# FFN stage on one NeuronCore: the quantised rows turned by DMA from SyncE instead of by TensorE through PSUM

## The chip, the cores and the metric

One core of a Trainium2 chip. The metric is the device time of one execution in microseconds (us); lower is better.

## The reference, cut to what matters

The whole program is an attention layer and, behind it, an expert layer with a quantised FFN, each with its residual. The change lies in the last stage only, which computes, for 4096 rows of 1024 values (`x` is the sum after attention):

```python
base   = x @ W.T                                   # 1024 x 1024
gates  = top-2 softmax of x @ Wr.T + language bias  # 8 experts, rank 16
z      = base + 2 * ((x @ A.T) * gates) @ B.T
zb     = z.astype(bfloat16)
qg, sg = dynamic_quant(zb, inv_gate)               # xs = zb * inv; scale = max|xs| / 127 per row
qu, su = dynamic_quant(zb, inv_up)                 # q = clip(round(xs / scale), -127, 127)
gate   = (qg @ w_gate.T) * sg * s_wgate            # 1024 -> 512
up     = (qu @ w_up.T) * su * s_wup
inter  = clip(silu(gate) * up, -10, 10).astype(bfloat16)
qi, si = dynamic_quant(inter, inv_inter)
out    = x + (qi @ w_down.T) * si * s_wdown        # 512 -> 1024
```

## The kernel before, in words

The kernel has three stages one after the other. The attention stage and the output projection take the first 1640 us or so of the span and are not touched. The last stage, `expert_ffn_block`, works on 32 tiles of 128 rows (`TILES`), and `tile_loop` (L1018 on) writes the same body for each engine: the first four bodies (t = 0 to 3) written out, then a hardware loop of seven rounds of four bodies, then three bodies that only drain. Body t works on four tiles at once, guarded by `has(k)`: `has(0)` is the router and the splitting of x of tile t, `has(1)` the linear layer of tile t-1, `has(2)` the quantisation and the gate and up products of tile t-2, `has(3)` everything behind them of tile t-3. The order of work on an engine is the order in which the body is written, and semaphores order the engines against each other. So each engine stands still at the first wait that isn't met, with all that follows in its body behind it.

The engines and the names that the change and the prediction touch:

- SyncE (SP) issues DMAs. In body t: wait for `fin_set`, store the result of tile t-3 (L1058), then load x of tile t+1 into one of four buffers (L1035). It has nothing else to do.
- ScalarE (ACT), in this order: `zb` from PSUM to bf16, in two halves (L1114); `Sigmoid` of the gate (L1118); `x_hi`, the high part of x of tile t (L1123), which waits for the load; for i = 0 and 1 (gate, up) the rounding `xs[i] * rinv + ROUND` (L1127) and the quantised rows `qb[i]`, 128 rows x 1024 values in bf16 (L1131); the two router weights `w12` (L1134, L1135); `qi` (L1139) and `qiT` (L1142) of the down product.
- VectorE (DVE), in this order: `gt` (L1185), `xs[0]` (L1192), `ut` (L1196), the maxima and scales of the rows (L1168 to L1178), the intermediate and its quantisation (L1210 to L1220, of them `xi` L1213), the router (L1223 to L1233), the clamp of the turned rows `qT[0]`, `qT[1]` (L1238), `hg_hi` and `hg_lo` (L1242, L1244), `diag` (L1248), the gates and `hg` (L1253 to L1260), `si_sb` (L1268), and the two products that make the output `o` (L1274, L1277).
- GpSimd (POOL): `xs[1]` (L1081), two products of silu (L1084, L1087), `x_lo` (L1090), the residual `fin` (L1094).
- TensorE (PE), in this order: the first half of the linear layer of tile t-1, 24 matmuls (L1291); router and LoRA of tile t (L1307); 6 matmuls of the second half; the 16 transposes of `qb` into `q_ps` (L1318); 6 matmuls; the transpose of `hg` (L1327); the transposes of `qi` (L1332), which wait for `qi_set`; 6 matmuls; the row scales (L1342), which wait for `diag_set`; the down product, 32 matmuls (L1348); 6 matmuls; the gate product of tile t-2 (L1357), which waits for `qT_set` and `o1_set`; the LoRA product (L1370); the up product (L1357).

`q_ps` is two of the eight banks of PSUM. `qT[i]` is laid out `[128, 8, 128]`: value, chunk of 128 values, row.

Of the kernel before, what the change touches and what calls it, by code (L numbers as in the profile page):

```python
# [21 lines left out]
BF16 = mybir.dt.bfloat16  # L22
I32 = mybir.dt.int32
U32 = mybir.dt.uint32
ALU = mybir.AluOpType
# [3 lines left out]
P = 128  # L29
# [3 lines left out]
C = D // P  # L33
TILES = POS // P
# [10 lines left out]
QMAX = 127.0  # L45
# [890 lines left out]
def expert_ffn_block(nc, ctx, io, x2T, out, ident, resident):  # L936
# [11 lines left out]
    def ps(name, shape, dt=F32):  # L948
        return ctx.enter_context(nc.psum_tensor(name, shape, dt))

    def sem(name):
        return ctx.enter_context(nc.semaphore("f_" + name))
# [10 lines left out]
    ident_b = sb("ident_b", [P, P], BF16)  # L963
# [15 lines left out]
    zb = sb("zb", [P, D], BF16)  # L979

    xs = [raw[:, i] for i in range(2)]
    qb = [sb(f"qb{i}", [P, D], BF16) for i in range(2)]
    qT = [sb(f"qT{i}", [P, C, P], BF16) for i in range(2)]

    amax, rinv = sb("amax", [P, 3], F32), sb("rinv", [P, 3], F32)
    sc = sb("sc", [P, 4, 3], F32)
# [5 lines left out]
    o_sb = [raw[:, 2 + i].rearrange("p (c n) -> p c n", n=P) for i in range(2)]  # L992

    z_ps = ps("z_ps", [P, 2, HALF])
    q_ps = ps("q_ps", [P, 2, C, P], BF16)
    g_ps = ps("g_ps", [P, 2, HALF])
    s_ps = ps("small_ps", [P, HALF])
    t_ps = ps("turn_ps", [P, HALF])
# [3 lines left out]
    x_in = [sem(f"x_in{i}") for i in range(4)]  # L1002
    (b_in, dn_in, vec_in, inv_in, o_out, w_hi_set, w_lo_set, b_hi_set, b_lo_set, ident_set, iota_set, lang_set, lbias_set,
     a_mm, xh_set, xl_set, lg_set, m8_set, ix_set, gap_set, ixf_set, w12_set, g1_set, g2_set, gates_set, hc_set, hg_set,
     ht_mm, hh_set, hl_set, z_mm, zb_set, xg_set, xu_set, amax_set, sc_set, rinv_set, rnd_set, qb_set, tq_mm,
     qT_set, gu_mm, gt_set, ut_set, sg_set, p1_set, p2_set, ib_set, xi_set, iamax_set, isc_set, irinv_set,
     ird_set, icl_set, diag_set, qi_set, ti_mm, qiT_set, si_mm, si_set, d_mm, o1_set, o2_set, fin_set) = (sem(n) for n in (
        "b_in", "dn_in", "vec_in", "inv_in", "o_out", "w_hi", "w_lo", "b_hi", "b_lo", "ident", "iota", "lang", "lbias",
# [3 lines left out]
        "ird", "icl", "diag", "qi", "ti_mm", "qiT", "si_mm", "si", "d_mm", "o1", "o2", "fin"))  # L1012

    UNROLL = 4
    block = ctx.enter_context(nc.Block())

    def tile_loop(eng, body):


        for j in range(UNROLL):  # L1020
            body(j, j, lambda k, j=j: k <= j)
        with eng.Fori(1, TILES // UNROLL) as T:
            for j in range(UNROLL):
                body(T * UNROLL + j, j, lambda k: True)
        for j in range(3):
            body(TILES + j, j, lambda k, j=j: k > j)
# [5 lines left out]
    @block.sync  # L1032
    def _(sp):
        def load_x(t, j):
            sp.dma_start(x_sb[j], x2T[:, :, bass.ds(t * P, P)].rearrange("c p n -> p c n")).then_inc(x_in[j], 16)  # L1035

        load_x(0, 0)
        sp.dma_start(b_raw[:], bT[:, :]).then_inc(b_in, 16)
        with nc.allow_non_contiguous_dma(reason="1024 scales, once"):
            sp.dma_start(sd_c[:], s_down.rearrange("(c p) -> p c", p=P)).then_inc(vec_in, 16)  # L1040
        def load_vector(dst, src, done):
            sp.dma_start(dst, src.rearrange("(o n) -> o n", o=1).broadcast_to([P, dst.shape[1]])).then_inc(done, 16)

        load_vector(lang_i[:], itok, vec_in)
        load_vector(sg_all[:], s_gate, vec_in)
        load_vector(su_all[:], s_up, vec_in)
        load_vector(ii_all[:], inv_inter, vec_in)
        load_x(1, 1)
        sp.wait_ge(w_lo_set, C)
        load_vector(ig_all, inv_gate, inv_in)  # L1050
        load_vector(iu_all, inv_up, inv_in)

        def body(t, j, has):
            if has(3):
                sp.wait_ge(fin_set, t - 2)
                if not (isinstance(t, int) and t == 3):
                    sp.wait_ge(o_out, t * 16 - 48)
                sp.dma_start(out[bass.ds(t - 3, 1)].rearrange("o p n -> (o p) n"),  # L1058
                             o_sb[(j + 1) % 2].rearrange("p c n -> p (c n)")).then_inc(o_out, 16)

            if has(0) and not (isinstance(t, int) and t == 0):
                load_x((t + 1) % TILES, (j + 1) % 4)

        tile_loop(sp, body)
        sp.wait_ge(o_out, 16 * TILES)
        sp.wait_ge(x_in[0], 16 * (TILES // 4 + 1))

# [31 lines left out]
    @block.scalar  # L1099
    def _(act):  # L1100
        act.wait_ge(x_in[0], 16)
        act.activation(x_hi[0][:], x_sb[0], ACT.Identity).then_inc(xh_set, 1)
        for c in range(C):
            act.activation(w_hi[:, c], raw[:, c], ACT.Identity).then_inc(w_hi_set, 1)
        act.wait_ge(b_in, 16)
        act.activation(b_hi[:], b_raw[:], ACT.Identity).then_inc(b_hi_set, 1)

        def body(t, j, has):
            if has(2):
                act.wait_ge(xg_set, t - 2)  # L1110
                act.wait_ge(xu_set, t - 2)
                for b in range(2):
                    act.wait_ge(z_mm, t * 2 - 3 + b)
                    act.activation(zb[:, b * HALF:(b + 1) * HALF], z_ps[:, b], ACT.Copy).then_inc(zb_set, 1)  # L1114
            if has(3):
                act.wait_ge(gt_set, t - 2)
                act.wait_ge(ib_set, t - 3)
                act.activation(silu[:], gt[:], ACT.Sigmoid).then_inc(sg_set, 1)  # L1118
            if has(0) and not (isinstance(t, int) and t == 0):
                act.wait_ge(x_in[j], x_count(t, j))  # L1120
                if not (isinstance(t, int) and t < 2):
                    act.wait_ge(z_mm, t * 2 - 2)
                act.activation(x_hi[j % 2][:], x_sb[j], ACT.Identity).then_inc(xh_set, 1)  # L1123
            if has(2):
                for i in range(2):
                    act.wait_ge(rinv_set, t * 2 - 3 + i)
                    act.activation(xs[i], xs[i], ACT.Copy, bias=ROUND, scale=rinv[:, i:i + 1]).then_inc(rnd_set, 1)  # L1127
                    if i == 0 and not (isinstance(t, int) and t == 2):
                        act.wait_ge(tq_mm, t * 2 - 4)
                    act.wait_ge(rnd_set, t * 2 - 3 + i)  # L1130
                    act.activation(qb[i][:], xs[i], ACT.Copy, bias=-ROUND).then_inc(qb_set, 1)  # L1131
            if has(0):
                act.wait_ge(gap_set, t + 1)
                act.activation(w12[:, 0:1], gap[:], ACT.Sigmoid)  # L1134
                act.activation(w12[:, 1:2], gap[:], ACT.Sigmoid, scale=-1.0).then_inc(w12_set, 1)  # L1135
            if has(3):
                act.wait_ge(icl_set, t - 2)
                act.wait_ge(ti_mm, t - 3)
                act.activation(qi[:], xi[:], ACT.Copy, bias=-ROUND).then_inc(qi_set, 1)  # L1139
                act.wait_ge(ti_mm, t - 2)  # L1140
                act.wait_ge(d_mm, t - 3)
                act.activation(qiT[:], qi_ps, ACT.Copy).then_inc(qiT_set, 1)  # L1142

        tile_loop(act, body)

    @block.vector
    def _(dve):
# [8 lines left out]
        for e in range(2):  # L1156
            rows = slice(SEQ * e, SEQ * (e + 1))
            ins = dve.tensor_copy(lang[rows, :], lang_i[rows, :].rearrange("p (t e) -> p t e", e=2)[:, :, e])
# [21 lines left out]
        def body(t, j, has):  # L1180
# [51 lines left out]
                dve.wait_ge(ix_set, t + 1)  # L1232
                dve.tensor_copy(ixf[:], ix[:, 0:2]).then_inc(ixf_set, 1)  # L1233
            if has(2):
                dve.wait_ge(gu_mm, t * 2 - 4)
                for i in range(2):
                    dve.wait_ge(tq_mm, t * 2 - 3 + i)
                    dve.tensor_scalar(qT[i][:], q_ps[:, i], QMAX, -QMAX, ALU.min, ALU.max).then_inc(qT_set, 1)  # L1238
            if has(1):
                dve.wait_ge(ht_mm, t)  # L1240
                dve.wait_ge(z_mm, t * 2 - 2)
# [40 lines left out]
    def _(pe):  # L1282
# [11 lines left out]
        def body(t, j, has):  # L1294
# [7 lines left out]
            if has(0):  # L1302
# [3 lines left out]
                for c in range(C):  # L1306
                    ins = pe.matmul(h_ps, x_sb[j][:, c, :], ar_w[:, c, :], start=(c == 0), stop=(c == C - 1))  # L1307
                ins.then_inc(a_mm, 1)
            if has(1):
                if not first:  # L1310
                    pe.wait_ge(zb_set, t * 2 - 2)
                linear(one, 1, range(0, 2), first)
            if has(2):
                pe.wait_ge(qT_set, t * 2 - 4)
                for i in range(2):
                    pe.wait_ge(qb_set, t * 2 - 3 + i)
                    for c in range(C):
                        ins = pe.transpose(q_ps[:, i, c], qb[i][:, c * P:(c + 1) * P], ident_b[:])  # L1318
                    ins.then_inc(tq_mm, 1)
            if has(1):  # L1320
                linear(one, 1, range(2, 4), first)
                pe.wait_ge(hg_set, t)
# [5 lines left out]
            if has(3):  # L1328
                pe.wait_ge(ut_set, t - 2)
                pe.wait_ge(qi_set, t - 2)  # L1330
                for c in range(CI):
                    ins = pe.transpose(qi_ps[:, c], qi[:, c * P:(c + 1) * P], ident_b[:])  # L1332
# [3 lines left out]
            if has(3):  # L1336
# [9 lines left out]
                for f in range(C):  # L1346
                    for c in range(CI):
                        ins = pe.matmul(g_ps[:, f // 4, (f % 4) * P:(f % 4 + 1) * P],  # L1348
                                        dn_w[:, c, f * P:(f + 1) * P], qiT[:, c], start=(c == 0), stop=(c == CI - 1))
# [14 lines left out]
            if has(1):  # L1364
# [3 lines left out]
                for b in range(2):  # L1368
                    for k, (a, w) in enumerate(((hg_hi, b_hi), (hg_hi, b_lo), (hg_lo, b_hi))):
                        ins = pe.matmul(z_ps[:, b], a[:], w[:, b * HALF:(b + 1) * HALF],  # L1370
                                        start=False, stop=(k == 2))
# [75 lines left out]
```

## Time and profile before

| | |
|---|---|
| time, median of 3 | 2393.21 us (2391.35 to 2397.13) |
| the profiled execution | 2398.05 us, span 2396.1 us |
| busy in the span | PE 95%, PEld 77%, DVE 55%, ACT 29%, POOL 55% |
| DMA | 188.33 MB, mean 79 GB/s |
| the chain that ended last | of the span: TensorE 11%, VectorE 6%, GpSimd 6%, issue 5%, ScalarE 2% |

Times are in us from the start of the span. PE is TensorE's matmuls, PEld its weight loads, SPq the queue of SyncE's DMA instructions. A bracket at the end of a line of the timeline is the idle time of the engine before that instruction and what ended it. The chain view goes back from the last instruction, at each step to what released it; a piece in it can be shorter than the instruction, since it ends where the next piece was released.

### The profile page before, as it was taken

What the parts mean: (1) busy time and instruction counts of PE and PEld (TensorE: products, weight loads), DVE (VectorE), ACT (ScalarE), POOL (GpSimd) and SP (SyncE); (2) the same over time, 40 slices, a digit from 0 to 9 for tenths busy, and PEclk for the clock granted to TensorE, in tenths of its full rate; (3) what the DMA queues carried; (4) which work ended last, traced back from release to release, by engine and by line L of the source; (5) the groups of instructions that cost most, each with busy time, mean ns of one, the idle gap of its engine ahead of it and who ended that gap; (6) DMA issues with size and microseconds to landing.
All of it is one profiled execution on the core that took longest, in us unless ns stands there. A gap on an engine that the chain in (4) does not pass through costs nothing. (4 is left out here: it accounts for less than half of the span.)

```text
span 2396.1 us, 48171 instructions
## 1 busy us (share of the span) xinstructions
PE 2268.3 (95%) x19520; PEld 1836.1 (77%) x19552; DVE 1307.3 (55%) x2248; ACT 701.5 (29%) x1122; POOL 1319.8 (55%) x1091
## 2 busy tenths in 40 slices
PE   6999999999999999999996999998999999999996
PEld 5888877888778888788885888886777777777774
DVE  5354464445644555545455322224677777777775
ACT  3222242222422223322223101012343333333332
POOL 6887878887778786888750000001455445445443
PEclk9999999999999999999998999998999999999998
DMA  4211122111221112121116844444011111111111
GB/s 139 65 60 57 61 98 68 63 59 63 80 89 56 66 54 72 65 69 54 63 37 202 239 165 132 132 166 132 19 53 53 39 49 53 47 41 53 53 35 44
DMA packets 130374, 188.33 MB, mean 79 GB/s; under 512 B 16162, under 2 KB 61346, under 8 KB 130210
## 3 DMA queue, kind: packets, MB, share of 16 engines
q1 hardware_dynamic: 118130, 165.92, 21.7%
q10 hardware_dynamic: 9216, 16.78, 1.8%
q0 software_dynamic: 2864, 3.28, 0.8%
q8 instruction: 123, 2.02, 0.3%
q14 instruction: 41, 0.34, 0.0%
HBM read 138.76 MB, written 50.33 MB: 79 GB/s over the span
## 5 line engine op out<-in xcount | busy, mean ns | idle before, releaser
L662 PE MATMUL acc<-y_hi,w_slot_hi 128*128 128x512 f32 x1344 | 541.6, 403 | 29.8 <-DVE unit L521 9.0
L662 PE MATMUL acc<-y_hi,w_slot_lo 128*128 128x512 f32 x1344 | 528.6, 393 | 0.0
L662 PE MATMUL acc<-y_lo,w_slot_hi 128*128 128x512 f32 x1344 | 527.7, 393 | 0.0
L313 POOL TENSOR_TENSOR w_slot_lo<-w_raw,w_slot_hi 128x512 fp32r<-128x512 f32 x329 | 424.3, 1290 | 26.3
L662 PEld LDWEIGHTS acc<-y_hi,w_slot_hi 128*128 128x128 f32 x1344 | 254.7, 189 | 90.2 <-issue 27.3
L311 POOL CAST w_slot_hi<-w_raw 128x512 fp32r<-128x512 f32 x329 | 218.0, 663 | 169.2 <-PE acc L662 134.8
L662 PEld LDWEIGHTS acc<-y_hi,w_slot_lo 128*128 128x128 f32 x1344 | 254.6, 189 | 54.8
L662 PEld LDWEIGHTS acc<-y_lo,w_slot_hi 128*128 128x128 f32 x1344 | 255.1, 190 | 48.9
L316 POOL TENSOR_TENSOR w_raw<-w_raw 128x512 f32<-128x512 f32 x188 | 259.4, 1380 | 25.6 <-DMA w_raw<-wu 20.5
L1094 POOL TENSOR_TENSOR raw<-raw,c_raw 128x1024 f32<-128x1024 f32 x32 | 76.2, 2380 | 347.0 <-DVE raw L1277 347.0
L1291 PE MATMUL z_ps<-w_hi,x_hi 128*128 128x512 f32 x512 | 219.1, 428 | 1.4 <-DVE w_lo L1150 1.2
L929 PE MATMUL o_ps<-c_hi,wo_hi 128*128 128x512 f32 x512 | 200.3, 391 | 10.7 <-DVE wo_lo L887 10.7
L511 DVE COPY cx<-att 128x512 f32<-128x512 f32 x63 | 43.6, 692 | 305.5 <-PE att L717 277.2
L1291 PE MATMUL z_ps<-w_hi,x_lo 128*128 128x512 f32 x512 | 202.2, 395 | 0.0
L1291 PE MATMUL z_ps<-w_lo,x_hi 128*128 128x512 f32 x512 | 200.8, 392 | 0.0
L929 PE MATMUL o_ps<-c_lo,wo_hi 128*128 128x512 f32 x512 | 200.1, 391 | 0.0
L929 PE MATMUL o_ps<-c_hi,wo_lo 128*128 128x512 f32 x512 | 200.1, 391 | 0.0
L521 DVE TENSOR_TENSOR unit<-acc,unit 128x512 f32<-128x512 f32 x144 | 98.8, 687 | 177.2 <-PE acc L662 172.8
L909 DVE SCALAR_TENSOR_TENSOR out_c<-o_ps,bo_c,x_c 128x512 f32<-128x512 f32 x64 | 48.1, 751 | 254.5 <-PE o_ps L929 174.5
L1070 POOL DMA_DIRECT2D dn_w<-wdT x1 | 0.8, 752 | 305.5 <-POOLq L1399 305.5
L504 DVE TENSOR_TENSOR prob<-prob,inv 128x512 f32<-128x512 f32 x126 | 156.4, 1241 | 4.3
L374 ACT ACTIVATE prob<-prob 128x512 f32<-128x512 f32 x126 | 72.7, 624 | 183.5 <-PE acc L662 171.7
(166 smaller groups left out, 3840.1 us busy)
## 6 DMA issues: line engine op xcount, KB each, us to landing
w_raw<-wu SPq DMA_DIRECT2D x192, 256.0 KB, 3.1
c_raw<-context_T SPq DMA_DIRECT2D x9, 2048.0 KB, 11.0
c_raw<-x_T SPq DMA_DIRECT2D x33, 512.0 KB, 4.6
x_c<-xT SPq DMA_DIRECT2D x64, 256.0 KB, 3.5
x_T<-out_c ACTq DMA_DIRECT2D x64, 256.0 KB, 3.7
out<-raw SPq DMA_DIRECT2D x32, 512.0 KB, 3.1
context_T<-cx SPq DMA_DIRECT2D x63, 256.0 KB, 3.5
x_raw<-x SPq DMA_DIRECT2D x27, 512.0 KB, 4.7
```

What stands on the lines that cost most here:

```text
L311: pool.tensor_copy(w_hi[:, k], raw).then_inc(w_hi_set, 1)
L313: pool.tensor_tensor(w_lo[:, k], raw, w_hi[:, k].bitcast(F32), ALU.subtract).then_inc(w_set, 1)
L316: pool.tensor_tensor(w_raw[:, dst], w_raw[:, a], w_raw[:, b], op).then_inc(w_mix, 1)
L374: act.activation(prob_of(n)[:, p], prob_of(n)[:, p], ACT.Exp, scale=SCALE).then_inc(exp_set, 1)
L504: dve.tensor_tensor(p3, p3, inv[:, p].unsqueeze(2).broadcast_to([P, 8, SEQ]), ALU.mult)\
L511: dve.tensor_copy(cx_of(n).rearrange("p (j e q) -> p e j q", e=2, q=SEQ), c_bank(n)[:, :, 0:HALF // 2].rearrange("p e (j q) -> p e j q", q ...
L521: dve.tensor_tensor(uo[U % 3][:, o], acc[:, a % 2], uo[U % 3][:, o], ALU.add).then_inc(dve_out, 1)
L662: ins = pe.matmul(bank, w[:, k, c, :], v[:, k, c, :], start=(k in (0, 1, 5) and c == 0 and i == 0), stop=(c == C // 2 - 1 and i == 2), ski ...
L909: dve.scalar_tensor_tensor(out_c[f % 2][:], o_ps[f % 4][:], bo_c[:, f:f + 1], x_c[f % 2][:], ALU.add, ALU.add).then_inc(x2_set, 1)
L929: ins = pe.matmul(o_ps[f % 4][:], w[:, c, f * P:(f + 1) * P], v[i][:, c], start=(c == 0 and k == 0), stop=(c == C - 1 and k == 2))
L1094: pool.tensor_tensor(o_sb[(j + 1) % 2], o_sb[(j + 1) % 2], x_sb[(j + 1) % 4], ALU.add)\
L1291: pe.matmul(z_ps[:, b], a[i][:, c, :], w[:, c, b * HALF:(b + 1) * HALF], start=(c == 0 and k == 0), stop=False)
```

## The change

In body t, SyncE waits until the gate and up products of the previous tile are done (`gu_mm`), then for `qb[0]` and issues a transposing DMA from `qb[0]` to `qT[0]`, then the same for `qb[1]`; its store and its load follow behind these. The transfers count up `turned[i]`. VectorE waits for `turned[i]` and clamps `qT[i]` in place, in SBUF. ScalarE waits for the previous tile's `turned[i]` ahead of each write of `qb[i]`. TensorE's 16 transposes and the PSUM tensor `q_ps` are gone. SyncE's bodies are written out, 35 of them, in place of the loop.

```diff
-    q_ps = ps("q_ps", [P, 2, C, P], BF16)
...
+    turned = [sem(f"turned{i}") for i in range(2)]
...
         def body(t, j, has):
+            if has(2):
+                if not (isinstance(t, int) and t == 2):
+                    sp.wait_ge(gu_mm, t * 2 - 4)
+                for i in range(2):
+                    sp.wait_ge(qb_set, t * 2 - 3 + i)
+                    sp.dma_start_transpose(qT[i][:], qb[i][:]).then_inc(turned[i], 16)
             if has(3):
                 sp.wait_ge(fin_set, t - 2)
...
-        tile_loop(sp, body)
+        for t in range(TILES + 3):
+            body(t, t % 4, lambda k, t=t: k <= t < TILES + k)
...
                     act.activation(xs[i], xs[i], ACT.Copy, bias=ROUND, scale=rinv[:, i:i + 1]).then_inc(rnd_set, 1)
-                    if i == 0 and not (isinstance(t, int) and t == 2):
-                        act.wait_ge(tq_mm, t * 2 - 4)
+                    if not (isinstance(t, int) and t == 2):
+                        act.wait_ge(turned[i], t * 16 - 32)
                     act.wait_ge(rnd_set, t * 2 - 3 + i)
...
             if has(2):
-                dve.wait_ge(gu_mm, t * 2 - 4)
                 for i in range(2):
-                    dve.wait_ge(tq_mm, t * 2 - 3 + i)
-                    dve.tensor_scalar(qT[i][:], q_ps[:, i], QMAX, -QMAX, ALU.min, ALU.max).then_inc(qT_set, 1)
+                    dve.wait_ge(turned[i], t * 16 - 16)
+                    dve.tensor_scalar(qT[i][:], qT[i][:], QMAX, -QMAX, ALU.min, ALU.max).then_inc(qT_set, 1)
...
-            if has(2):
-                pe.wait_ge(qT_set, t * 2 - 4)
-                for i in range(2):
-                    pe.wait_ge(qb_set, t * 2 - 3 + i)
-                    for c in range(C):
-                        ins = pe.transpose(q_ps[:, i, c], qb[i][:, c * P:(c + 1) * P], ident_b[:])
-                    ins.then_inc(tq_mm, 1)
```

## Rows read from the trace of the kernel before

**Rows 1.** The page, part 1: busy time by engine.

```profile
PE 2268.3 (95%) x19520; PEld 1836.1 (77%) x19552; DVE 1307.3 (55%) x2248; ACT 701.5 (29%) x1122; POOL 1319.8 (55%) x1091
```

**Rows 2.** One period: us, PE, PEld, DVE, ACT, POOL busy, clock, DMA share, GB/s

```profile
1893.00:1915.17 22.17, 21.46 (x142) 16.50 (x142) 16.95 (x35) 8.37 (x13) 10.58 (x6) 1.00 0.16 47
```

**Rows 3.** Waits, 28 tiles: who <- whom, us, times, longest.

```profile
ACT x_hi L1123 <- DMA c_raw<-x_T: 131.1, 28, 4.9
...
PE g_ps L1332 <- ACT qi L1139: 7.0, 27, 0.4
```

**Rows 4.** Chain that ended last, from one zb to the next.

```profile
1892.69 0.61 ACT zb L1114
...
1899.79 2.79 DVE xi L1213
...
1905.66 0.53 ACT qi L1139
...
1906.32 0.38 PE g_ps L1332 x4
...
1908.37 1.79 PE g_ps L1348 x32
...
1914.88 0.61 ACT zb L1114
```

**Rows 5.** Timeline (start, us, engine, line): transposes, clamps, diag, row scales.

```profile
1902.98 0.62 PE L1318 MATMUL q_ps<-ident_b,qb 128*128 128x128 bf16 x8
...
1903.88 0.62 PE L1318 MATMUL q_ps<-ident_b,qb 128*128 128x128 bf16 x8 [0.28 <-ACT qb L1131]
...
1904.31 0.48 PE L1291 MATMUL z_ps<-w_hi,x_hi 128*128 128x512 f32 x1
...
1905.59 1.29 DVE L1238 TENSOR_SCALAR qT<-q_ps 128x1024 bf16<-128x1024 bf16 x2
...
1907.32 0.28 DVE L1248 TENSOR_SCALAR diag<-ident,sc 128x128 f32<-128x128 f32 x1
...
1907.99 0.38 PE L1342 MATMUL turn_ps<-diag,ones 128*128 128x128 f32 x2
```

**Rows 6.** Timeline: quantised rows, addition, store, load, x_hi.

```profile
1902.77 1.06 ACT L1131 ACTIVATE qb<-raw 128x1024 bf16<-128x1024 f32 x1
...
1912.83 2.38 POOL L1094 TENSOR_TENSOR raw<-raw,c_raw 128x1024 f32<-128x1024 f32 x1 [10.81 <-DVE raw L1277]
...
1915.48 0.37 SPq L1058 DMA_DIRECT2D out<-raw  x1
...
1916.05 0.38 SPq L1035 DMA_DIRECT2D c_raw<-x_T  x1
...
1920.61 1.06 ACT L1123 ACTIVATE x_hi<-c_raw 128x1024 fp32r<-128x1024 f32 x1 [4.62 <-DMA c_raw<-x_T]
```

**Rows 7.** DMA issues, whole span: KB each, median us to landing.

```profile
c_raw<-x_T SPq DMA_DIRECT2D x33, 512.0 KB, 4.6
...
out<-raw SPq DMA_DIRECT2D x32, 512.0 KB, 3.1
...
context_T<-unit SPq DMA_DIRECT2D x1, 256.0 KB, 2.0
...
ar_w<-wrT SPq DMA_DIRECT2D x1, 32.0 KB, 11.2
```

**Rows 8.** Timeline of TensorE: idle times in brackets, and the last tiles.

```profile
20.37 0.80 PE L623 MATMUL att<-wc_raw,unit 128*128 128x128 f32 x5 [2.46 <-DVE y_lo L524]
...
383.32 0.47 PE L662 MATMUL acc<-y_hi,w_slot_hi 128*128 128x512 f32 x1 [2.39 <-ACT unit L412]
...
2368.19 3.27 PE L1348 MATMUL g_ps<-qiT,dn_w 128*128 128x128 bf16 x32
```

**Rows 9.** Stretches after the idle times of rows 8, columns as rows 2.

```profile
20.40:23.80 3.40, 3.40 (x31) 3.40 (x31) 3.11 (x6) 2.87 (x7) 3.40 (x4) 1.00 0.09 27
...
383.90:387.20 3.30, 3.30 (x10) 2.55 (x9) 1.82 (x4) 0.00 (x0) 3.08 (x4) 0.58 0.00 0
```

More of the change, by code:

```diff
@@ L1004, in expert_ffn_block @@
      a_mm, xh_set, xl_set, lg_set, m8_set, ix_set, gap_set, ixf_set, w12_set, g1_set, g2_set, gates_set, hc_set, hg_set,
-     ht_mm, hh_set, hl_set, z_mm, zb_set, xg_set, xu_set, amax_set, sc_set, rinv_set, rnd_set, qb_set, tq_mm,
+     ht_mm, hh_set, hl_set, z_mm, zb_set, xg_set, xu_set, amax_set, sc_set, rinv_set, rnd_set, qb_set,
      qT_set, gu_mm, gt_set, ut_set, sg_set, p1_set, p2_set, ib_set, xi_set, iamax_set, isc_set, irinv_set,
```

2 rows, old and new, of the table x_in are left out of this document.

## The prediction

> **What bounds the kernel now.** The page first: TensorE is busy for 95% of the span [rows 1], which invites the sum "less work on TensorE, less time". So I went on to the stretches, one period of the tile loop by itself: 22.17 us, TensorE busy for 21.46 of them, at full clock, the DMA engines at a share of 0.16 [rows 2]. What matters is the 0.7 us in which TensorE stands still: it says whether it follows something. The waits, from 1720 to 2340 us (28 tiles), show that it does: before the transposes of `qi` it waits for ScalarE 27 times, 7.0 us in all, 0.26 us each; and ScalarE's `x_hi` waits 4.7 us per tile for the load of x [rows 3]. Last the chain of waits, from one `zb` to the next (1892.69 to 1914.88): `zb`, GpSimd, VectorE's `xi` and what follows it, `qi`, and only then TensorE, at 1906.32, which it then stays on through the down, gate and LoRA products to the next `zb` [rows 4]. One period of it is 22.19 us, the period of the loop. The linear layer's first half, the router product and the transposes of `qb` are not in it: TensorE does them while the others carry the chain, and has them done 0.26 us too early. The stage is bound by a ring of engines, with TensorE close behind.
>
> **What the change takes away.** Sixteen transposes of a tile: from 1902.98 to 1904.31, when the linear layer goes on, 1.33 us, of which 0.28 us is a wait for the second `qb` [rows 5]. In 32 tiles that is 43 us of TensorE's time. All of it lies ahead of the `qi` transposes, which start when `qi` ends (1905.66 + 0.53 = 1906.19, the transposes at 1906.32 [rows 4]). `qi` depends on nothing that was removed. So TensorE comes 1.33 us earlier to the same wait, which grows from 0.26 to about 1.6 us, and the gain is nothing. The cover is that wait: were `qi` early, the 1.33 us would count.
>
> **What it adds.** VectorE's clamps now wait for a transfer that can begin only when `qb` is written. The first `qb` ends about 2.13 us ahead of the second (the spacing of their rounding and copying, 1.06 us and a like instruction), the second at 1902.77 + 1.06 = 1903.83 [rows 6]. Until now VectorE took up both clamps at 1905.59, when it was through with the router, and `diag` ended at 1907.60, in time for TensorE's row scales at 1907.99 [rows 5]. With L as the time from the issue of the second transfer until it has landed, the clamp starts at 1903.83 + 0.27 + L (0.27 us is how late SyncE reacts: `fin` ends at 1915.21, its store is issued at 1915.48 [rows 6]). That passes 1906.2, the start of the second clamp now, from L = 2.1 us. Behind the waiting clamp on VectorE are queued `hg_hi`, `hg_lo`, `diag`, the gates, `si_sb` and both output products; TensorE's row scales wait for `diag`, and the down product stands behind them.
>
> That closes a new ring, whose pieces all have rows. From the end of `fin` (1915.21) over SyncE's store and load to the start of `x_hi` (1920.61): 5.40. From there to the end of the second `qb` (one tile earlier: 1898.44 to 1903.83): 5.39. SyncE's reaction 0.27, L, one clamp 0.65 (two take 1.29), from there to the end of `diag` 0.72 (1906.88 to 1907.60), the hand-over to TensorE 0.14 (as from `qi` [rows 4]), from the row scales (1907.99) to the end of `fin` (1915.21) 7.22 [rows 5, 6]. Sum: 19.79 + L. The old ring of 22.17 holds up to L = 2.4 us; beyond, each us of L is a us of each tile.
>
> L is the unknown; no transposing DMA is in this trace. Lower end: a store of 256 KB, the same bytes, by itself: 2.0 us. Then a store of 512 KB at 3.1, and the load of x at 4.6 [rows 7]; this load is of 1024 pieces (128 rows x 8 chunks), as the transpose has 1024 runs of 128 values, though with twice the bytes. Upper end: 1024 pieces of 32 bytes (the router's eight columns, queued behind other loads) took 11.2 us [rows 7]; a turned block is likewise written in short pieces. I take 4.6, by the number of pieces. The ring is then 24.39, +2.22 us a tile. I count 30 tiles (bodies 3 to 31, and one for the two draining bodies in which the rows are still turned; the first body has nothing behind it): +67 us.
>
> Then the clock. TensorE would stand still for about 2.2 us at the row scales in each tile. The trace has six idle times of 2.3 to 3.0 us in the attention stage; after five of them the granted clock was near 0.5 (1.2 GHz) for a stretch, as after the one that ended at 383.32 (0.58 over 383.90 to 387.20), after the one that ended at 20.37 it stayed at 1.00 [rows 8, 9]. The down product at half clock took 3.27 us against 1.79 [rows 8, 4]: +1.5, and it is on the ring. 2.2 us is at the low end of those idle times, so I count half of the tiles: 0.5 x 1.5 x 30 = +23 us. The bounds are 0 and +45.
>
> Small edits. The clamp in SBUF has no row in its form: between free (0.65 us off the ring, 20 us in all) and as long as from PSUM, 0.65 each [rows 5]; I take the latter, since the elements are the same. SyncE's waits stand ahead of its store and load, but `qb` is ready 11.4 us before `fin`, so nothing is late unless the issue of two transposes takes that long. The wait of ScalarE for the previous tile's `turned` is met a period earlier. SyncE's bodies without a loop: nothing. PSUM saved: nobody waits for it.
>
> One rule against a row. The trace shows transfers of 256 and 512 KB at 2.0 to 4.6 us [rows 7]. The Trainium skill, "DMA: Bandwidth & Descriptors", section on latency and other measured facts, gives a transposing DMA about 350 to 400 GB/s when contiguous, 261 in one kernel; as an estimate 256 KB are then 0.7 to 1.0 us beside the fixed part, near the lower end, and the sum by it would be within 30 us of the time before. No row here shows it.
>
> **The sum.** Against the profiled execution, 2398.05 us (span 2396.1 and 1.95 around it): 2398.05 + 67 + 23 = 2488. That execution is 4.8 us above the median of 2393.21, so 2483 as a median.
>
> **The rivals.**
> - *Quick crossbar, no change.* L of 2.0 to 2.4: the second clamp is in time, the old ring stays at 22.17, TensorE only waits longer for `qi`. For it: the store of 256 KB. Against it: that is the fastest transfer of its size here. 2393 us. Chance 0.05. With L from 2.4 to 3.1 the loss is up to 0.72 x 30 = 22 us, 2394 to 2415: chance 0.07.
> - *The forecast*, L of 3.1 to 6.5: ring 22.9 to 26.3, with or without the clock's part: 2415 to 2393 + 124 + 45 = 2562. Chance 0.60.
> - *Slow transpose.* L of 6.5 to 11.2: ring up to 31.0, +265 and the clock's 45: 2562 to 2703. For it: the short pieces of a turned block. Chance 0.17.
> - *Transposes in a queue.* The second is issued 2.13 us after the first. If one occupies the crossbar for D over 2.13, the second waits for it, and L becomes 2.0 + 2D - 2.13. If D is the upper row less the lower one, 9.2, L = 18.3, the ring 38.1, +15.9 x 30 = +477: 2870 us. Against it: the same row had a queue of other loads ahead. Chance 0.08, with the change lowered into element-wise copies counted in. The Trainium skill, "VectorE: DVE Perf Modes", section "The three transpose paths", has 1309 ns for one 128x128 square by the crossbar against 390 for TensorE: it speaks against this change. Eight squares in a row would be an estimate of 10.5 us for a transfer, and the sum by it about 2950.
> - *Faster: TensorE sets the period after all.* Place: TensorE's own order between the router product and the `qi` transposes. If the 0.26 us wait for `qi` is an artefact of modelled ends, and the transfers land before VectorE asks, the period falls by 1.33: 2393 - 1.33 x 32 = 2350 us. It decides as long as L is under 2.1 us and `qi` comes with TensorE. Against it: the wait is there 27 times out of 28, and the chain passes by the transposes. Chance 0.03.
>
> **How the numbers follow.** A measurement of this kernel tells 0.3%, 7 us, from nothing. Faster 0.03; within 7 us 0.06 (the quick crossbar and the edge of the next case); slower 0.91. The likeliest time is 2483. The range must leave out no more than 0.2: from 2405 (leaving some 0.1 below) to 2700 (leaving some 0.1 above, the queue and the end of the slow case).
>
> **What would show it.** Steps right: TensorE's wait before L1332 at about 1.6 us; VectorE idle ahead of the second clamp, ended by a DMA; a TensorE wait for `diag` of about 2 us that was not there; a period of 22.17 + (L - 2.4), with L read off the issue of the transposes; granted clock under 1.00 in the last stage. Wrong: a period under 22 us, which would mean that the chain was misread; a second transfer that lands more than 2.2 us after the first, which means the queue; SyncE's store or load late, which would mean that the issue of a transpose itself is long.

## The result and the profile after

| | before | after |
|---|---|---|
| time, median of 7 | 2393.21 us | 2402.66 us (2399.69 to 2404.15) |
| ratio to before | 1 | 1.0036, 95% interval 1.0021 to 1.0051 |
| the profiled execution | 2398.05 us, span 2396.1 us | 2404.15 us, span 2402.0 us |
| one period of the tile loop, mean of 27 | 22.21 us | 22.43 us |

The changed kernel is slower by 0.36%, 5 to 12 us by the interval. The prediction was 2483 us with a range from 2405: the direction is right, the size is not. The periods are taken from the start of one `xs[1]` on GpSimd to the next, from the fourth tile on. They grow by 0.23 us each, 6.2 us in 27 tiles, where the two spans differ by 5.9 us.

The page of the kernel after, parts 1 and 3, beside [rows 1]: TensorE has lost 30 us of busy time, and the first queue has 67584 packets more.

```profile
PE 2238.1 (93%) x19008; PEld 1811.5 (75%) x19040; DVE 1296.4 (54%) x2248; ACT 701.4 (29%) x1122; POOL 1323.4 (55%) x1091
...
q1 hardware_dynamic: 185714, 182.71, 25.5%
```

The stretches of after, columns as in [rows 2]: us, PE, PEld, DVE, ACT, POOL busy, clock, DMA share, GB/s. A usual period comes first, in which TensorE is busy for 20.51 us against 21.46 of 22.17 before; then one period at 0.93 of the clock.

```profile
1893.00:1915.50 22.50, 20.51 (x126) 15.61 (x126) 16.50 (x36) 8.34 (x13) 10.63 (x5) 1.00 0.28 70
2273.00:2297.00 24.00, 22.00 (x126) 17.26 (x126) 16.77 (x35) 8.43 (x13) 10.62 (x6) 0.93 0.26 66
```

The waits of after, 1720 to 2340 us, 28 tiles, beside [rows 3]:

```profile
ACT x_hi L1131 <- DMA c_raw<-x_T: 120.8, 27, 4.7
...
PE g_ps L1332 <- ACT qi L1147: 48.2, 28, 1.9
...
DVE qT L1245 <- DMA qT<-qb: 20.6, 28, 1.0
...
PEld turn_ps L1342 <- DVE diag L1255: 7.4, 23, 0.5
```

TensorE's wait ahead of the transposes of `qi` has gone from 0.26 to 1.72 us a tile. That is where the removed work went: into waiting. Two waits are new: VectorE for the transfer, 0.74 us a tile, and TensorE's weight load for `diag`, 0.3 us each in 23 tiles.

The transfers in the timeline of after, beside [rows 5, 6], and under them the rows of the view of the tile `qT`:

```profile
1901.23 3.38 SPq L1060 DMA_TRANSPOSE qT<-qb  x2
...
1902.29 1.06 ACT L1139 ACTIVATE qb<-raw 128x1024 bf16<-128x1024 f32 x1
...
1905.15 0.43 DVE L1245 TENSOR_SCALAR qT<-qT 128x1024 bf16<-128x1024 bf16 x1
...
1905.86 0.38 PE L1332 MATMUL g_ps<-ident_b,qi 128*128 128x128 bf16 x4 [1.70 <-ACT qi L1147]
...
1906.43 0.43 DVE L1245 TENSOR_SCALAR qT<-qT 128x1024 bf16<-128x1024 bf16 x1 [0.85 <-DMA qT<-qb]
...
1907.63 0.49 PE L1342 MATMUL turn_ps<-diag,ones 128*128 128x128 f32 x2
```

```profile
L1060 SPq DMA_TRANSPOSE qT<-qb x64: 1231/1232/1367, 1680.0 to 2369.8; - x64
L1245 DVE TENSOR_SCALAR qT<-qT x64: 418/427/431, 1683.3 to 2372.9; 128x1024 bf16<-128x1024 bf16 x64
...
DMA to landing us min/median/max: 3.0/3.0/3.2
```

The second `qb` ends at 1903.35. The two issues, 3.38 us together with what lies between, end at 1904.61, so the second begins at 1903.38, 0.03 us after `qb`. It lands 3.0 us later, and the second clamp starts at 1906.43. L, the time from the start of the issue to the landing, is 3.0 us, in all 64 cases within 3.0 to 3.2. The clamp in SBUF takes 0.43 us.

The chain that ended last now has the new ring in it in some periods (here one of them, from the store to the clamp), in others still the old one:

```profile
1934.95 2.39 POOL raw L1102
1937.35 0.35 SPq L1065
...
1937.74 5.02 DMA c_raw<-x_T
...
1943.75 1.14 ACT raw L1135
...
1947.17 1.07 ACT qb L1139
1948.25 3.05 DMA qT<-qb
```

### The profile page after: what moved, and what is told of

It is laid out like the page before. It is cut to its first block and busy times, and to the rows that moved or that the text cites. A ratio compares the mean times of both kernels' runs of the same rounds, so it can differ in the third digit from the quotient of the medians.

```text
span 2402.0 us, 47066 instructions
## 1 busy us (share of the span) xinstructions
PE 2238.1 (93%) x19008; PEld 1811.5 (75%) x19040; DVE 1296.4 (54%) x2248; ACT 701.4 (29%) x1122; POOL 1323.4 (55%) x1091
## 3 DMA queue, kind: packets, MB, share of 16 engines
q1 hardware_dynamic: 185714, 182.71, 25.5%
## 5 line engine op out<-in xcount | busy, mean ns | idle before, releaser
L316 POOL TENSOR_TENSOR w_raw<-w_raw 128x512 f32<-128x512 f32 x188 | 258.8, 1377 | 26.2 <-DMA w_raw<-wu 22.3
```

The lines of the kernel that those rows point to most:

```text
L316: pool.tensor_tensor(w_raw[:, dst], w_raw[:, a], w_raw[:, b], op).then_inc(w_mix, 1)
```

## The experiments

Theory R is the prediction's: a ring of engines sets the period, TensorE's removed 1.33 us lie beside a wait, and the second transfer has closed a ring a little longer than the old one. The rivals: S, the transfers cost by what they do beside everything (queues, loads, SyncE's written-out bodies); T, TensorE's time counted and the transfers took back more. A time is compared with the runs of the kernel before that were made with it. The periods, means over 27 tiles from the fourth on (25 at `e6_twice`), stand in the table; each is from the one profiled execution of its kernel, the ratios (with 95% intervals) are from all executions.

| kernel | ratio to before | period, us |
|---|---|---|
| after | 1.0036 (1.0021 to 1.0051) | 22.43 |
| e1_late | 1.0020 (1.0009 to 1.0031) | 22.25 |
| e7_beside | 1.0007 (0.9997 to 1.0017) | 22.22 |
| e8_half | 0.9999 (0.9988 to 1.0011) | 22.25 |
| e2_before_late | 0.9996 (0.9983 to 1.0009) | 22.20 |
| e6_twice | 1.0534 (1.0509 to 1.0559) | 26.22 |
| e5_after_xlo | 1.0014 (1.0002 to 1.0025) | 22.30 |
| e4_before_xlo | 0.9953 (0.9939 to 0.9968) | 21.77 |
| e10_before_icl | 0.9978 (0.9969 to 0.9988) | 22.02 |
| e12_before_hg | 0.9922 (0.9908 to 0.9935) | 21.75 |
| e3_late_xlo | 0.9889 (0.9872 to 0.9905) | 21.36 |
| e9_best | 0.9977 (0.9968 to 0.9986) | 22.06 |
| e11_xlo_hg | 0.9898 (0.9883 to 0.9913) | 21.52 |
| e13_xlo_si | 0.9808 (0.9790 to 0.9826) | 20.51 |

**The transfer off the ring.** `e1_late` moves the clamps down VectorE's order, from ahead of `hg_hi`, `hg_lo` and `diag` to behind `hg` and ahead of `si_sb`:

```diff
-            if has(2):
-                for i in range(2):
-                    dve.wait_ge(turned[i], t * 16 - 16)
-                    dve.tensor_scalar(qT[i][:], qT[i][:], QMAX, -QMAX, ALU.min, ALU.max).then_inc(qT_set, 1)
...
+            if has(2):
+                for i in range(2):
+                    dve.wait_ge(turned[i], t * 16 - 16)
+                    dve.tensor_scalar(qT[i][:], qT[i][:], QMAX, -QMAX, ALU.min, ALU.max).then_inc(qT_set, 1)
```

> The changed kernel, with VectorE's two clamps moved behind diag, the gates and hg, directly ahead of si_sb. Theory R (the ring through the second transfer, fin, store, load, x_hi, qb, transfer, clamp, diag, down product, sets 22.4 us a tile; TensorE's removed 1.33 us are worth nothing because it waits for qi): the transfer leaves the ring, the old ring stays, period 22.2, time 2390 to 2396 us, no wait for diag at L1342 and no wait of VectorE for a transfer ahead of it. Rival S (the 9 us come from what the transfers do beside: loads delayed, or SyncE's written-out bodies): stays at 2402. Rival T (TensorE's 1.33 us counted, and the transfer took back more than that): with the transfer off the path, 2350 to 2360.

Measured 2396.74 us, the period back to 22.25. In its waits neither VectorE's wait for a DMA nor the wait for `diag` is left, and TensorE waits for `qi` as long as in the changed kernel:

```profile
PE g_ps L1332 <- ACT qi L1147: 48.2, 28, 1.9
ACT w L1142 <- DVE gap L1238: 47.7, 28, 1.9
```

T is out: with the transfer off the path no 40 us appear. The period went where R says. The interval of the ratio stays above 1, though, by 2 to 7 us, of which the period accounts for 1; no row shows what the rest is.

**The side effects.** `e7_beside` leaves TensorE's transposes and the clamps as before, writes SyncE's bodies out, and adds both transfers into scratch tiles; only ScalarE's next write of `qb` waits for them:

```diff
+                for i in range(2):
+                    sp.wait_ge(qb_set, t * 2 - 3 + i)
+                    if not (isinstance(t, int) and t == 2):
+                        sp.wait_ge(turned[i], t * 16 - 32)
+                    sp.dma_start_transpose(qs[i][:], qb[i][:]).then_inc(turned[i], 16)
...
-        tile_loop(sp, body)
+        for t in range(TILES + 3):
+            body(t, t % 4, lambda k, t=t: k <= t < TILES + k)
```

> The kernel before, with SyncE's bodies written out and both transposing transfers issued beside everything into scratch tiles that only ScalarE's next write of qb waits for; TensorE's transposes stay. Theory R: nothing on the ring, 2390 to 2396 us. Rival S: the side effects alone, 2402.

2394.84 us, 1.0007: S is out as the cause, for all side effects taken together. The load of x lands in 4.8 us instead of 4.6 here too, as in the changed kernel, and the period doesn't show it.

**One transfer.** `e8_half` turns `qb[0]` by DMA and `qb[1]` by TensorE, with its clamp from PSUM:

```diff
-                for i in range(2):
+                for i in range(1):
                     sp.wait_ge(qb_set, t * 2 - 3 + i)
                     sp.dma_start_transpose(qT[i][:], qb[i][:]).then_inc(turned[i], 16)
...
+                for c in range(C):
+                    ins = pe.transpose(q_ps[:, 1, c], qb[1][:, c * P:(c + 1) * P], ident_b[:])
```

> The changed kernel with only the gate rows (qb[0]) turned by a DMA and the up rows (qb[1]) by TensorE's 8 transposes and the clamp from PSUM, as before. Theory R: the first transfer is written 2.2 us before the second and landed at 1904.2 where its clamp starts at 1905.15, so it is hidden: period 22.2, 2390 to 2397 us. Rival: each transfer costs its share, half of the 9 us: 2398.

2395.23 us. The first transfer by itself costs nothing that the interval (0.9988 to 1.0011) would show; the price is the second's. `e2_before_late` is the control for moving the clamps, in the kernel before:

> The kernel before with VectorE's two clamps from PSUM moved ahead of si_sb, the transposes left with TensorE. A control for the move by itself. Theory R: diag comes 1.3 us earlier to a TensorE that waits for qi, nothing changes: 2390 to 2396 us. If the move alone gave or cost something, the late clamps of the changed kernel would have to be read against that.

2394.67 us, as expected: in the kernel before the move by itself is worth nothing.

**The slope and the clock.** `e6_twice` does the second transfer twice, one after the other:

```diff
                     sp.dma_start_transpose(qT[i][:], qb[i][:]).then_inc(turned[i], 16)
+                    if i == 1:
+                        sp.wait_ge(turned[1], t * 32 - 48)
+                        sp.dma_start_transpose(qT[i][:], qb[i][:]).then_inc(turned[i], 16)
...
```

> The changed kernel with the second transposing transfer done twice, one after the other has landed; VectorE and ScalarE wait for the second. Theory R: L grows by 3.1 us, the period from 22.4 to 25.5, +3.1 x 30 = 93 us: 2495 us with TensorE at full clock; TensorE then stands about 3 us at the row scales in each tile, and by the clock step of the prediction (1.5 us for a down product at half clock) up to 45 us more, 2540. Rival S: the transfers cost by their number only, 2402 + 5 = 2407. The granted clock in the last stage decides on the clock step.

2522.07 us, +128. The ring with L = 6.1 is 25.4; the mean period is 26.2. The excess of 0.8 us comes in lumps. Taken from the end of one `fin` to the next, 25 rounds of the ring fall in two groups: 8 take 25.2 to 25.5 us, which is the ring as summed, and 17 take 25.9 to 27.1 us. In the longer ones the down product takes longer. Here one of them, the view of the timeline and then the stretch that begins with it; the down product takes 3.48 us against 1.95 a tile earlier:

```profile
1891.71 1.95 PE L1351 MATMUL g_ps<-qiT,dn_w 128*128 128x128 bf16 x32
...
1915.48 0.43 DVE L1248 TENSOR_SCALAR qT<-qT 128x1024 bf16<-128x1024 bf16 x1 [3.56 <-DMA qT<-qb]
...
1916.68 0.80 PE L1345 MATMUL turn_ps<-diag,ones 128*128 128x128 f32 x2 [2.46 <-DVE diag L1258]
...
1917.27 3.48 PE L1351 MATMUL g_ps<-qiT,dn_w 128*128 128x128 bf16 x32
```

```profile
1917.00:1920.80 3.80, 3.80 (x35) 3.74 (x35) 0.68 (x4) 0.00 (x0) 0.00 (x0) 0.54 0.00 0
```

The prediction's clock step, half of the tiles at 1.5 us each, is 0.75 us a tile; measured are 0.8 to 0.9 us a tile, from 17 of 25 rounds at some 1.3 us each, after waits of 2.65 us on average (63.5 us in 24 tiles) where the prediction had 2.2. The average came out, the two factors less so. In the changed kernel there is no such wait for `diag`, and a down product at a lower clock came once in the loop (3.15 us against 1.95), in the period of 23.95 us.

**What the old ring consists of.** In the loop `xi` takes 2.79 us [rows 4], beside GpSimd's `x_lo`. In the draining bodies of the kernel before, where there is no `x_lo`, the timeline has it at 0.69:

```profile
2363.33 0.69 DVE L1213 TENSOR_TENSOR xi<-ib,ii_all 128x512 f32<-128x512 bf16 x1
```
`e4_before_xlo` lets `x_lo`, which TensorE wants only in the next body, wait for `xi`, in the kernel before:

```diff
             if has(0):
+                if has(3):
+                    pool.wait_ge(xi_set, t - 2)
                 pool.wait_ge(xh_set, t + 1)
```

> The kernel before with one wait more: GpSimd's x_lo (L1090) starts only when VectorE's xi (L1213) is done. In the trace xi takes 2.78 us beside x_lo and 0.69 us in the last tile, without it. Theory Q: GpSimd and VectorE hold each other up there, and this is 2.1 us of the old ring; the ring falls to 20.1, TensorE's own order becomes the bound at 22.17 - 0.26 = 21.9, time about 2385. Rival: the 2.1 us are not on the ring, or x_lo comes too late for TensorE: 2393 or more.

2382.89 us, period 21.77: as expected, with TensorE's wait for `qi` gone from the list of waits. What is left there is 0.3 us a tile for the second `qb`, ahead of its transposes. The same wait in the changed kernel, clamps left where they are (`e5_after_xlo`) and clamps late (`e3_late_xlo`):

> The changed kernel with the x_lo wait alone, the clamps where the change has them. Theory R: the ring through the transfer has neither xi nor x_lo in it and stays at 22.3 to 22.4: 2397 to 2403 us, against 2383 for the same wait in the kernel before; so the change would cost 17 us there. Rival: the slower time of the changed kernel comes from the old ring (xi, qi) becoming longer: then this falls as the kernel before did, to 2391.

> The changed kernel with both moves: VectorE's clamps ahead of si_sb, and GpSimd's x_lo only behind VectorE's xi. Theory: transfer and hold-up are both off the ring, so now TensorE's order or ScalarE's is the bound. TensorE would be at 21.75 - 1.33 = 20.4 us; ScalarE comes to qi only behind the second qb and w12, some 1.2 us earlier than now, a ring of 21.0. Period 21.0, time 2393 - 1.2 x 30 = 2357, at most 2340. That is where the removed transposes count: against the kernel before with the x_lo wait alone (2383) about 25 us less. Rival: TensorE's transposes never were worth anything, 2383 as without them.

`e5_after_xlo` took 2399.02 us: the new ring has no `xi` in it and the period falls by 0.13 us only, from 22.43 to 22.30. TensorE now waits for `diag`, and the changed kernel is 16 us behind `e4_before_xlo`, where without the wait on `xi_set` it is 9 behind the kernel before. With the clamps late, 2368.86 us, 1.1% below before, but 12 us above what was expected. Its timeline shows why: `x_lo` now holds up the next operation on `xi`:

```profile
1910.90 2.42 POOL L1100 TENSOR_TENSOR x_lo<-c_raw,x_hi 128x1024 fp32r<-128x1024 f32 x1 [1.35 <-DVE xi L1223]
...
1911.89 1.72 DVE L1228 TENSOR_SCALAR xi<-xi,rinv 128x512 f32<-128x512 f32 x1
```

I then pushed `x_lo` further back, behind `icl_set`, the last operation on `xi` (`e9_best`, and `e10_before_icl` in the kernel before), behind `hg_set` (`e11_xlo_hg`, `e12_before_hg`), and at last behind `si_set` (`e13_xlo_si`); each of these runs has one of the three added lines:

```diff
-                    pool.wait_ge(xi_set, t - 2)
+                    pool.wait_ge(icl_set, t - 2)
+                    pool.wait_ge(hg_set, t + 1)
+                    pool.wait_ge(si_set, t - 2)
```

> The changed kernel with the clamps ahead of si_sb and x_lo only behind VectorE's last operation on xi (icl_set in place of xi_set). In the run with xi_set the hold-up had moved to the next operation on xi (L1228 there, 1.72 us against 0.49). Theory: with it gone the ring falls by another 1.2 us to 20.1, and TensorE's own order is the bound at 21.75 - 1.33 = 20.4 to 20.6: period 20.5, time 2369 - 0.85 x 30 = 2344 us. Rival: ScalarE's order (second qb, w12, qi) holds the ring at 21.3, 2366.

> The kernel before with the same wait on icl_set. Theory: it is bound by TensorE's own order already with the wait on xi_set (21.75), so nothing more comes: 2380 to 2386 us. The difference to the changed kernel with the same wait and late clamps is then what TensorE's 1.33 us are worth where nothing else sets the period: 1.2 to 1.33 x 30 = 36 to 40 us. Rival: it falls with the ring as well, and the transposes on TensorE are still worth less than half of that.

Both were misses: 2391.14 and 2389.8 us. The hold-up moved to `gap`, a subtraction of one value per row, which is on the way to `w12` and `qi`:

```profile
1916.47 2.43 POOL L1100 TENSOR_TENSOR x_lo<-c_raw,x_hi 128x1024 fp32r<-128x1024 f32 x1 [3.44 <-DVE xi L1230]
1916.63 0.16 DVE L1237 MAX8 m<-lg 128x8 f32<-128x8 f32 x1
1916.82 2.09 DVE L1240 TENSOR_TENSOR gap<-m 128x1 f32<-128x1 f32 x1
```

> The changed kernel with the clamps ahead of si_sb and x_lo only behind hg. In the run with icl_set the hold-up had moved on to gap, an operation of one value per row (2.09 us against 0.16). Behind hg stand only the two clamps and si_sb, which have some 2 us to spare. Theory: nothing between xi and qi is held up, the ring falls to 20.1 and TensorE's own order (21.75 - 1.33) is the bound: period 20.4 to 20.6, time 2391 - 1.5 x 30 = 2346 us. Rival: the hold-up moves on to the output product or to si_sb and the ring stays at 21.3 to 22.0: 2366 to 2390.

> The kernel before with the same wait on hg_set. Theory: bound by TensorE's own order with its transposes, period 21.75, 2380 to 2386 us; the difference to the changed kernel with the same wait is then the worth of the removed transposes, 36 to 40 us. Rival: the transposes on TensorE are worth less, and this kernel falls as low.

`e12_before_hg` has a period of 21.75 and took 2378.55 us; TensorE waits in it only for the second `qb`, 0.3 us a tile. `e11_xlo_hg` took 2373.47, its rival's band: now the two late clamps, in SBUF, stood beside `x_lo` (2.97 us for both in place of 0.85), and the output product behind them came late to TensorE's gate product, 36.2 us in 28 tiles. Whether the product itself would be held up, with one input in PSUM, `e13_xlo_si` tells, the clamps still ahead of `si_sb`:

> The changed kernel with the clamps ahead of si_sb and x_lo only behind si_sb, so that it runs beside the output products, of which the first reads PSUM. If an operation that reads PSUM is not held up: nothing between xi and the first product is, the ring falls and TensorE's own order is the bound, 20.4 to 20.6 us a tile, 2369 - 0.8 x 30 = 2345 us. If it is: the first product ends up to 1.2 us later, period 21.2 to 21.7, 2363 to 2380.

```profile
1889.90 0.28 DVE L1277 COPY si_sb<-turn_ps 128x128 f32<-128x128 f32 x1
1890.34 2.40 POOL L1100 TENSOR_TENSOR x_lo<-c_raw,x_hi 128x1024 fp32r<-128x1024 f32 x1 [8.35 <-DVE si_sb L1277]
1891.38 1.23 DVE L1283 TENSOR_TENSOR raw<-g_ps,si_sb 128x1024 f32<-128x1024 f32 x1 [1.19 <-PE g_ps L1350]
...
1903.10 0.69 DVE L1223 TENSOR_TENSOR xi<-ib,ii_all 128x512 f32<-128x512 bf16 x1
...
1904.93 0.49 DVE L1228 TENSOR_SCALAR xi<-xi,rinv 128x512 f32<-128x512 f32 x1
...
1906.39 0.16 DVE L1240 TENSOR_TENSOR gap<-m 128x1 f32<-128x1 f32 x1
```

It isn't: 1.23 us, as ever, and the period is 20.51 us, the time 2347.95, 1.9% below the kernel before. TensorE's own order is the bound there. Against `e12_before_hg`, which has the transposes on TensorE, the periods differ by 1.24 us, the medians by 31 us or 1.0 us a tile (the profiled execution of `e12_before_hg` was the slowest of its five, 2386.09 us). So 1.0 to 1.24 us a tile is what the removed transposes are worth where the ring doesn't cover them; expected were 36 to 40 us. The two kernels also differ in where `x_lo` waits: a kernel before with the wait on `si_set` wasn't run.

The Trainium skill, "SBUF — State Buffer", section "Who interferes with whom", states a rule for this: VectorE and GpSimd share a pair of ports under an exclusive lock, which VectorE wants for two inputs in SBUF or in its two-port modes, and an operation with at most one SBUF input outside these modes doesn't contend. The traces agree in who is held up: `xi`, `gap` (two inputs in SBUF), L1228 and the clamps (single input) were, until `x_lo` ended, the product that reads PSUM was not. They don't show the ports themselves.

**What L goes by.** `e14_sizes` issues transposes beside the kernel before: of `qb[0]` two halves of 512 columns in a row, of `qb[1]` the first 128 columns.

```diff
+                    if i == 0:
+                        sp.dma_start_transpose(qs[0][:, 0:4], qb[0][:, 0:HALF]).then_inc(turned[0], 16)
+                        sp.dma_start_transpose(qs[0][:, 4:8], qb[0][:, HALF:D]).then_inc(turned[0], 16)
+                    else:
+                        sp.dma_start_transpose(qs[1][:, 0:1], qb[1][:, 0:P]).then_inc(turned[1], 16)
```

> The kernel before with transposing DMAs beside it into scratch tiles: of qb[0] its two halves of 512 columns, issued one right behind the other, and of qb[1] its first 128 columns. Nothing waits for them but the next write of qb. If L goes by a fixed part, all land about 2.0 to 2.5 us from their issue, the 128 columns not much sooner than 512. If it goes by bytes or blocks (3.0 for 1024 columns, a floor of 2.0 from the fastest store): 128 columns 2.1, 512 columns 2.5, and SyncE is busy 1.23 us with 1024 columns, 0.6 with 512, 0.15 with 128. Time within 7 us of before.

The view by source line, 32 issues each (SyncE's time for one in ns, min/median/max; then from issue to landing), for the first half, the second half and the 128 columns:

```profile
L1062 SPq DMA_TRANSPOSE qs<-qb x32: 1201/1202/1660, 1676.5 to 2358.2; - x32
DMA to landing us min/median/max: 2.4/2.4/2.8
...
L1063 SPq DMA_TRANSPOSE qs<-qb x32: 1188/1259/1267, 1677.9 to 2359.5; - x32
DMA to landing us min/median/max: 2.4/2.5/2.6
...
L1065 SPq DMA_TRANSPOSE qs<-qb x32: 1176/1182/1234, 1679.2 to 2360.8; - x32
DMA to landing us min/median/max: 2.3/2.3/2.3
```

2.3 us for 32 KB, 2.4 for 128 KB (2.5 for the second half, which was issued while the first was still under way), 3.0 for 256 KB, and SyncE is busy 1.2 us with each. L is for the most part fixed, and 0.1 to 0.7 us of it goes by size. Of the two expectations the first was nearer; SyncE's time was expected to fall with the size and doesn't. The time, 2393.69 us, is a single one beside 2394.58.

## Why the prediction was wrong, point by point

**What bounds the kernel: right.** The chain passes by the transposes; `e1_late`, `e8_half` and `e2_before_late` stay within 0.2% of the time before, and the transposes are worth 1.0 to 1.24 us a tile only when the ring is shortened (`e13_xlo_si` against `e12_before_hg`). The case "TensorE sets the period after all" is refuted.

**What is taken away: right in size and place.** The wait ahead of L1332 was to be about 1.6 us, it is 1.72.

**The new ring: right in its course, the bounds of its pieces near.** With the measured pieces it is 19.79 less 0.22 for the clamp (0.43 against 0.65) less 0.24 for SyncE's reaction (0.03 against 0.27), plus 3.0: 22.33, where the two rings, now nearly equal, give 22.43 with the one slow period, 22.38 without. The other pieces moved a little too and cancel out. The medians of 25 rounds in the loop of the changed kernel are: from `fin` to `x_hi` 5.23 (5.40 in the prediction), to the end of the second `qb` 5.45 (5.39), from there to the clamp 3.09 (0.27 + 4.6), the clamp 0.43 (0.65), to the end of `diag` 0.72 (0.72), the hand-over 0.06 (0.14), to the end of `fin` 7.33 (7.22), together 22.31. `e6_twice` has the slope: 25.2 to 25.5 us where the clock holds.

**L: the step that failed.** I took 4.6 us, the row of the load of x, because its number of pieces is that of the transpose's runs. Measured 3.0. That makes 1.6 of the 2.22 us a tile, 48 of the 67 us. The number of pieces was right (the queue has 1056 packets more for each transfer, 0.25 KB each on average), but the time doesn't go by it: `e14_sizes` has 2.3 us for 128 columns against 3.0 for 1024, eight times as much. Nearer rows were there. In [rows 7] it is the store of 512 KB at 3.1, or the store of 256 KB at 2.0: with what SyncE needs longer for the issue (1.23 against 0.35 us, known only from the run after) it comes to 2.9. The page of the kernel before also has 383 transfers of 256 KB in the attention stage and the output projection, which the prediction left out:

```profile
w_raw<-wu SPq DMA_DIRECT2D x192, 256.0 KB, 3.1
...
x_c<-xT SPq DMA_DIRECT2D x64, 256.0 KB, 3.5
x_T<-out_c ACTq DMA_DIRECT2D x64, 256.0 KB, 3.7
...
context_T<-cx SPq DMA_DIRECT2D x63, 256.0 KB, 3.5
```

The load of x has twice the bytes and a store issued 0.57 us ahead of it; which of its differences makes it slower no run tells. The Trainium skill's bandwidth (350 to 400 GB/s, "DMA: Bandwidth & Descriptors", section "Latency and other measured facts") pointed that way: as an estimate it left 0.7 us for 256 KB beside the fixed part, and 0.7 us separate 32 KB from 256 KB here. The 1309 ns that the Trainium skill's "VectorE: DVE Perf Modes", section "The three transpose paths", gives for one square don't add up over squares: in the runs eight squares cost 0.7 us more than one. Nor is there a queue of transposes: the second transfer lands in 3.0 us like the first.

**The reaction and the clamp: 0.46 us too much.** SyncE's 0.27 us between `fin` and the store was taken for its reaction; in the changed kernel both reactions are 0.03 us, also that to `fin` (1915.08 to 1915.11). It is the loop: in `e7_beside`, the kernel before with SyncE's bodies written out, `fin` ends at 1909.32 (1906.94 and 2.38) and the store is issued 0.03 us later, the load 0.40 us behind it. In `e2_before_late`, whose SyncE keeps its loop, it ends at 1909.23, and the same two are 0.27 and 0.56 us. The two issues in the one and then in the other, from the timelines:

```profile
1909.35 0.35 SPq L1066 DMA_DIRECT2D out<-raw  x1
1909.75 0.43 SPq L1037 DMA_DIRECT2D c_raw<-x_T  x1
```

```profile
1909.50 0.37 SPq L1058 DMA_DIRECT2D out<-raw  x1
1910.06 0.38 SPq L1035 DMA_DIRECT2D c_raw<-x_T  x1
```

The prediction had written the bodies out at no gain or cost, and kept the reaction of the loop for them. The clamp I left at its PSUM price; in SBUF it takes two thirds. At L = 3.0 the ring as I summed it would have been 22.79 and the loss 0.62 x 30 = 19 us; with these two it is 22.33, and 5 us. Measured are 9.

**The clock: a price near the measured one, a wrong premise.** The 2.2 us wait at `diag` never came about, since L was small; there is one slow period, worth 1.6 us, instead of 15 and 23 us. `e6_twice` has such a wait, and there the step holds on average.

**The range.** Its lower end, 2405, is L = 2.8 in the ring as summed. L came out just above that, and the 0.46 us of the other two pieces carried the time past the end. L between 2.4 and 3.1 had a chance of 0.07, although two of the three plain transfers shown lay at 2.0 and 3.1, and those left out at 3.1 to 3.7: the values around 3 should have had the most, and the pieces of the ring a spread of their own.

## What to carry to other kernels

Work taken off the busiest engine pays only if the chain of waits runs through it; look for the wait just behind it, which will swallow it, and shorten the ring first. A transfer that takes the place of an engine's work was priced here better by the plain transfers of its size (2.0 to 3.7 us in the trace, 3.0 measured) than by one with as many pieces (4.6), and what it costs depends on who is queued behind its landing: with the consumer late in its engine's order the loss fell from 0.36% to 0.20%, and the ring through the transfer was gone. An operation that takes four times as long in the loop as in the last tile is worth a look at its neighbours: here GpSimd held it up, and moving GpSimd's operation beside a product that reads PSUM gave the time back.

## What the runs showed of the hardware that was not expected

A transposing DMA from SBUF to SBUF takes SyncE 1.18 to 1.26 us to issue whether it turns 128 or 1024 columns of 128 rows, and lands 2.3, 2.4 and 3.0 us after the start of its issue for 128, 512 and 1024 columns. It adds 1056 packets to the queue for each transfer of 1024 columns (67584 in 64). With two of them in each period the median landing of a plain load of 512 KB goes from 4.6 to 4.8 us. SyncE issues 0.03 us after the operation that it waits for where its bodies are written out, and 0.25 to 0.28 us after it in its loop. GpSimd's `x_lo` of 2.4 us stops a VectorE operation of one value per row as long (2.09 us against 0.16) as one of 512 (2.79 against 0.69).
